# An adaptive layer and a routed feed-forward in one kernel: a third row buffer, another order of GpSimd's transfers, and no memsets between them

## The chip, the cores and the metric

One core of a Trainium2 chip. The time is that of one execution on the device, in microseconds (us), as median of several runs. The profile is one execution recorded by the hardware profiler; its times count from the span's start. Five engines work at the same time, each along its own queue of instructions: TensorE (PE), VectorE (DVE), ScalarE (ACT), GpSimd (POOL) and SyncE (SP). Semaphores alone order them.

## The reference

```python
def _L0_cond_ref(x, u, v, b, W, fc_bias):          # x (16, 512, 512); u = v (16, 1, 512, 16)
    z1 = einsum('bfi,bir->bfr', x, v[:, 0]) / inch
    z = einsum('bfr,bor->bfo', z1, u[:, 0]) / r
    return gelu(einsum('bfi,oi->bfo', x, W) + fc_bias + z + b)

def _L0_ffn_ref(x, w_router, b_router, w1, b1, w2, b2):   # 16 blocks of 128, 4 chosen for a row
    prob = softmax(xf @ w_router + b_router)
    _, idx = top_k(prob, 4)
    mask = (idx[:, :, None] == arange(16)).any(axis=1)
    h = relu(einsum('nd,ebd->neb', xf, w1b) + b1b)
    return einsum('neb,ebd,ne->nd', h, w2b, mask) + b2

x = x + _L0_ffn_ref(_L0_cond_ref(x, ...), ...)
```

There are 8192 rows of 512 numbers, all float32. A row's hidden values are needed for its four chosen blocks ("experts") alone.

## The kernel before

The rows are worked in 16 batches of 512, each in four quarters of 128 rows, so 64 steps. A step's layer (`layer`, three products of rounded high and low parts in place of a float32 product) ends in a PSUM bank; ScalarE takes it through gelu into a row buffer, `grow`. TensorE turns it (`turn_batch`), multiplies with the router's weights (`router`, partial sums over four chunks of 128 channels, which stand in four groups of 32 partitions), and for each batch the logits are copied to SBUF (`logits`) and turned to rows of tokens (`turn_logits`). VectorE chooses four experts for each row (`choose`, `choose_rest`), TensorE counts ahead of each row how many went to its expert (`ranks`), and VectorE makes from this the four places of the row in the experts' lists (`place`, semaphore `v_ix`).

GpSimd then scatters the row to its four places in DRAM (`place_rows`, tensor `xg`): four indirect DMAs for a quarter, each of 128 rows of 528 words (512 numbers, the row's number and other places). A row buffer may be overwritten when its scatters have landed (`s_sc`).

The lists are cut into tiles of 512 rows of one expert: 49 full tiles and 23 of two halves of 256, 72 in all. Tile `j` is loaded by SyncE from `xg` as soon as the batches that must be complete for it have landed (`load_tile`, `unlocked_by`): tile 41 needs batch 14, tile 45 batch 15. TensorE turns it (`turn_tile`), multiplies with the expert's first weights (`ffn1`, result `hid`), ScalarE and VectorE make from it the two parts of the hidden layer (`hh`, `hl`), and TensorE multiplies with the second weights (`ffn2`). ScalarE (even quarters) and VectorE (odd ones) copy the results out of PSUM into a result buffer `yss[n]` (`result`), and GpSimd scatters them, four indirect DMAs for a tile, into `yt` (`send`). A result buffer is free when its tile's scatters have landed (`s_y`).

All engines walk the same steps `s`. Step `s` does the layer of quarter `s` (to 63), the first product of tile `s - 30` and the second of tile `s - 31`; GpSimd in its step `s` places quarter `s - 7` and sends tile `s - 32`. The stages are thus: layers alone (steps 0 to 29), layers and tiles (30 to 63), tiles alone (64 to 102), and at the end VectorE adds four parts and `x` for each row, while SyncE loads and stores.

What stands in whose place in SBUF matters here. There are two row buffers `grow[0]` and `grow[1]`; the first six batches also use a third one in the space of `ys`. Result buffers 0 and 1 are `ys`, buffer 2 is `yspare` (in the space of the low parts of experts 8 to 11, `w2l[:, 8:12]`) up to tile 40, buffer 3 is `stx` from tile 36 on, buffers 4 and 5 are `grow[0]` and `grow[1]` from tiles 39 and 43 to 54, when batches 14 and 15 have been scattered. A tile takes of the free buffers the one longest unused. Up to tile 45 (`PRE`) the second weights are split for each tile; later tiles use splits of all experts (`presplit_w2`), which VectorE and ScalarE make two at a time in steps 67 to 72, 75 and 76, in the order of `PRESPLIT`.

Between two indirect DMAs of GpSimd stands a memset (`rest`), which waits for the memset before it. It writes 320 words a partition of `w2l[:, 15]`, or, in late steps, the small tile `rep`; expert 15's low part can be written only when 412 of them are done. From step 77 on there is instead one small memset after the second transfer of a tile, and a wait for it (`stop`).

```python
first = s <= LAG + 2 or q != 3
if 0 <= s - 7 < SLOTS and first:
    place_rows((s - 7) // 4, (s - 7) % 4)
if 0 <= j < NTILE:
    for c in range(chunks(j)):
        send(j, c)
if 0 <= s - 7 < SLOTS and not first:
    place_rows((s - 7) // 4, (s - 7) % 4)
```

## Time and profile before

| | us |
|---|---|
| median of 3 runs | 1148.82 (1147.45 to 1150.53) |
| the profiled execution | 1149.37 |
| its span | 1147.6 |
| TensorE busy | 865.1 (75%) |
| VectorE busy | 861.7 (75%) |
| GpSimd busy | 727.4 (63%) |
| ScalarE busy | 581.1 (51%) |

The time of an execution holds 1.8 us outside the span. Busy time says little by itself: TensorE has nothing to do in the last stage, the sums, which begin at about 933 us and last for the rest of the span.

### The profile page before, as it was taken

To read this page: it belongs to the slowest core of one execution; us is meant where nothing else is said; L and a number is where in the kernel's file an instruction comes from. 1 tells how busy PE (TensorE), PEld (TensorE's weight loads), DVE (VectorE), ACT (ScalarE), POOL (GpSimd) and SP (SyncE) were. 2 spreads that over 40 slices of the span, in tenths; PEclk is the share of its full clock that TensorE was granted. 3 is DMA by queue.
4 is the path that set the end of the run, shared out by engine and by line. 5 is a ranking of instruction groups with operands and counts; after the bars stand their busy time and mean duration, and the time that the engine had idled before them with its cause. 6 is when DMAs were issued, how large, how long until landed. Compare 5 with 4: busy or idle time off the path is not lost.

```text
span 1147.6 us, 18685 instructions
## 1 busy us (share of the span) xinstructions
PE 865.1 (75%) x4893; PEld 682.7 (59%) x4893; DVE 861.7 (75%) x2175; ACT 581.1 (51%) x1061; POOL 727.4 (63%) x1038
## 2 busy tenths in 40 slices
PE   8989989999999999999999876999999930000000
PEld 7757767777777776777777655788888820000000
DVE  4556666777687767767778974878998759987777
ACT  6535545756676575657657753766667610000000
POOL 1588888888888888888888897555555530000000
PEclk9989989999999999999999997999999965555555
DMA  6798679988899888988778887689987589999999
GB/s 188 262 330 299 236 270 334 310 293 298 288 314 305 289 285 300 312 282 297 265 276 313 302 289 262 245 296 342 317 282 243 192 313 425 425 427 429 426 432 378
DMA packets 103241, 354.88 MB, mean 309 GB/s; under 512 B 29961, under 2 KB 29961, under 8 KB 92384
## 3 DMA queue, kind: packets, MB, share of 16 engines
q1 hardware_dynamic: 59616, 217.22, 55.0%
q0 software_dynamic: 43424, 136.37, 30.3%
q8 instruction: 41, 0.67, 0.2%
q14 instruction: 64, 0.52, 0.1%
q10 hardware_dynamic: 96, 0.10, 0.0%
HBM read 200.47 MB, written 169.65 MB: 323 GB/s over the span
## 4 chain that ended last, share of the span: by engine, by line
PE 50%; DVE 14%; POOL 12%; DMA 11%; issue 7%; ACT 3%; another core or an unknown queue 2%; ACTq 0%; POOLq 0%; DVEq 0%; SPq 0%
PE lay L1185 12%; DMA w2l<-yt 9%; PE yps L1327 9%; PE hid L1294 8%; PE trn L1279 7%; POOL yt L563 4%; POOL xg L544 4%; PE hid L1299 4%; POOL w2l L528 3%; DVE stx L1040 3%; PE hid L1171 2%; PE trn L1206 2%; ACT gsb L643 2%; DMA outT<-ys 2%
## 5 line engine op out<-in xcount | busy, mean ns | idle before, releaser
L544 POOL DMA_INDIRECT xg<-grow,ix x224 | 226.7, 1012 | 70.2 <-issue 36.4
L817 DVE TENSOR_TENSOR gsb<-trn,gsb 128x512 fp32r<-128x512 f32 x239 | 162.4, 687 | 127.3 <-ACT gsb L643 75.2
L563 POOL DMA_INDIRECT yt<-ys,ids x170 | 176.7, 1039 | 72.6 <-issue 35.8
L1185 PE MATMUL lay<-w2l,xs 128*128 128x512 f32 x768 | 194.3, 403 | 0.0
L1279 PE MATMUL trn<-idf,gr 128*128 128x128 f32 x956 | 147.3, 277 | 27.0 <-DVE gsb L817 12.9
L1185 PEld LDWEIGHTS lay<-w2l,xs 128*128 128x128 f32 x768 | 144.6, 192 | 30.1
L528 POOL MEMSET w2l<- 128x320 f32 x412 | 161.3, 392 | 0.1
L1279 PEld LDWEIGHTS trn<-idf,gr 128*128 128x128 f32 x956 | 115.8, 142 | 68.3 <-DVE gsb L817 22.9
L643 ACT ACTIVATE gsb<-trn 128x512 fp32r<-128x512 f32 x239 | 142.6, 597 | 26.5 <-PE trn L1279 15.2
L1294 PE MATMUL hid<-gsb,w1c 128*128 128x512 f32 (+1 forms) x576 | 133.1, 374 | 11.9 <-ACT gsb L643 10.2
L671 ACT ACTIVATE hv<-hid,b1c 128x512 f32<-128x512 f32 (+1 forms) x94 | 52.6, 584 | 155.4 <-PE hid L1299 53.0
L1327 PE MATMUL yps<-w2c,hh 128*128 128x512 f32 x330 | 118.6, 441 | 3.1 <-DVE hl L1008 2.1
L1294 PEld LDWEIGHTS hid<-gsb,w1c 128*128 128x128 f32 x576 | 95.2, 192 | 39.3 <-ACT gsb L643 22.9
L1299 PE MATMUL hid<-gsb,w1c 128*128 128x512 f32 (+1 forms) x288 | 68.9, 362 | 3.8 <-DVE gsb L817 3.8
L626 ACT ACTIVATE grow<-lay 128x512 f32<-128x512 f32 x56 | 33.5, 598 | 66.1 <-PE lay L1190 43.6
L1327 PE MATMUL yps<-w2c,hl 128*128 128x512 f32 x165 | 65.8, 399 | 0.0
L563 POOL DMA_INDIRECT yt<-stx,ids x40 | 43.1, 1077 | 26.2 <-issue 9.5
L563 POOL DMA_INDIRECT yt<-yspare,ids x52 | 52.7, 1013 | 8.6 <-issue 8.1
L1299 PEld LDWEIGHTS hid<-gsb,w1c 128*128 128x128 f32 x288 | 50.4, 193 | 12.5 <-DVE gsb L817 4.2
L1327 PEld LDWEIGHTS yps<-w2c,hh 128*128 128x128 f32 x330 | 50.3, 193 | 7.3 <-DVE hl L1008 3.5
L795 DVE TENSOR_TENSOR xs<-stx,xs 128x512 fp32r<-128x512 f32 x64 | 44.1, 694 | 12.2 <-ACT xs L599 9.7
L635 ACT ACTIVATE stx<-trn 128x512 f32<-128x512 f32 x64 | 38.1, 595 | 30.0 <-remote 13.4
(243 smaller groups left out, 1823.9 us busy)
## 6 DMA issues: line engine op xcount, KB each, us to landing
gr<-xg SPq DMA_DIRECT2D x49, 1056.0 KB
xs<-yt SPq DMA_DIRECT2D x16, 2048.0 KB, 19.5
w2l<-yt SPq DMA_DIRECT2D x15, 2048.0 KB, 19.5
gr<-xg SPq DMA_DIRECT2D x45, 528.0 KB
stx<-xT SPq DMA_DIRECT2D x64, 256.0 KB, 4.3
outT<-ys SPq DMA_DIRECT2D x31, 512.0 KB, 20.4
xg<-xrow SPq DMA_DIRECT2D x16, 528.0 KB
w2f<-xrow SPq DMA_DIRECT2D x16, 512.0 KB
```

The source lines that it names most:

```text
L528: pool.memset(idle, 0.0).then_inc(g_pace, 1)
L544: pool.indirect_dma_start(out=xg, out_offset=bass.IndirectOffsetOnAxis(ap=ix[:, row_buffer(b), q, k:k + 1], axis=0), in_=grows[row_buffer( ...
L563: pool.indirect_dma_start(out=yt, out_offset=bass.IndirectOffsetOnAxis(ap=ids[:, j % 8, c:c + 1], axis=0), in_=yss[result_buffer(j)][:, c, ...
L643: act.activation(gsb[:, :, HI, c * P:(c + 1) * P], turned[TURN_BANK[n]][:, :].rearrange("p (k t) -> p k t", k=KC), ACT.Copy).then_inc(a_tn, 1)
L671: act.activation(hv[:, h * n:(h + 1) * n], hid[:, h * n:(h + 1) * n], ACT.Relu, bias=b1c[:, bass.DynSlice(e[h], 1)]).then_inc(a_hv, 1)
L795: dve.tensor_tensor(xs[:, b % 2, :, LO, cols], stx[:, x_buffer(s), :].rearrange("p (k t) -> p k t", k=KC), xs[:, b % 2, :, HI, cols].bitca ...
L817: dve.tensor_tensor(gsb[:, :, LO, c * P:(c + 1) * P], turned[TURN_BANK[n]][:, :].rearrange("p (k t) -> p k t", k=KC), gsb[:, :, HI, c * P: ...
L1185: pe.matmul(lay[s % 2][:, :], xs[:, b % 2, k, h, cols], wls[:, k, a, :], start=(k == 0 and a == HI and h == HI), stop=False)
L1279: last = pe.transpose(turned[TURN_BANK[n]][:, k * P:(k + 1) * P], gr[:, j % 2, c, k * P:(k + 1) * P], idf[:, :])
L1294: pe.matmul(hid[:, cols], w1x[h][:, a, k * P:(k + 1) * P], gsb[:, k, HI, cols], start=(h == 0 and k == 0 and a == HI), stop=False)
L1299: last = pe.matmul(hid[:, cols], w1x[h][:, HI, k * P:(k + 1) * P], gsb[:, k, LO, cols], start=False, stop=(h == len(parts) - 1 and k == KC ...
L1327: last = pe.matmul(second_out[RESULT_BANK[n]][:, :], hx[:, c * P:(c + 1) * P], w[a], start=(i == 0), stop=(i == 2))
```

## The change

The third row buffer (`grow3`) is there for all batches, so batch `b` is in buffer `b % 3`. It takes the space of the low parts of experts 11 to 14. The third result buffer is gone from there for tiles 0 to 33; `grow[1]` becomes one for tiles 34 to 54 (batch 13 was its last), `stx` from tile 36, the space of `grow3` for tiles 36 to 39 (now called buffer 5), `grow[0]` for tiles 39 to 54 (buffer 4, batch 15 was its last). GpSimd sends results ahead of rows in steps 33 to 66 and rows ahead of results before and after. Its memsets are gone up to step 76; the last three tiles have no pause either. The logits are turned by transposes of 128x128 with the identity `idf` into a whole bank, and VectorE sums the four chunks; before, a product with a matrix of ones (`sumk`) turned and summed at once. `PRE` is 47, and the splits for all experts go in the order 0 to 15.

```diff
-PRE = 46
-SPARE = 40
-MORE = 36, 39, 43, 55
+PRE = 47
+MORE = 34, 36, 39, 55
+SPARE = 36, 40
@@ row_buffer
-    return b % 3 if b < 6 else b % 2
+    return b % 3
@@ result_buffers
-        free = [0, 1] + [2] * (j <= SPARE) + [3] * (j >= MORE[0])
-        free += [4] * (MORE[1] <= j < MORE[3]) + [5] * (MORE[2] <= j < MORE[3])
+        free = [0, 1] + [2] * (MORE[0] <= j < MORE[3]) + [3] * (j >= MORE[1]) + [4] * (MORE[2] <= j < MORE[3])
+        free += [5] * (SPARE[0] <= j < SPARE[1])
@@ adaln_ffn
-        yspare = nc.alloc_sbuf_tensor_at("yspare", [P, 4, D], F32, offset=w2l_at + 8 * D * 4)
+        grow3 = nc.alloc_sbuf_tensor_at("grow3", [P, 4, W], F32, offset=w2l_at + 11 * D * 4)
+        yspare = nc.alloc_sbuf_tensor_at("yspare", [P, 4, D], F32, offset=w2l_at + 11 * D * 4)
-        yss = (ys[:, 0, :, :], ys[:, 1, :, :], yspare, stx, grow[:, 0, :, 0:D], grow[:, 1, :, 0:D])
+        yss = (ys[:, 0, :, :], ys[:, 1, :, :], grow[:, 1, :, 0:D], stx, grow[:, 0, :, 0:D], yspare)
@@ gpsimd
-            def rest(s):
-
-                if paced[0] > 0:
-                    pool.wait_ge(g_pace, paced[0])
-                idle = w2l[:, NE - 1, 0:REST].bitcast(F32) if s < SLOTS + 7 else rep[:, :, :].rearrange("p q e -> p (q e)")
-                pool.memset(idle, 0.0).then_inc(g_pace, 1)
-                paced[0] += 1
@@ place_rows
-                    rest(4 * b + q + 7)
@@ send
-                if j + LAG + 2 < PACED:
-                    rest(j + LAG + 2)
-                elif c == 1:
+                if j + LAG + 2 >= PACED and c == 1 and j < NTILE - 3:
                     stop()
@@ gpsimd's steps
-                first = s <= LAG + 2 or q != 3
+                first = s <= LAG + 2 or SLOTS + 3 <= s
@@ result, on scalar (and likewise on vector)
-                elif result_buffer(j) > 3:
-                    b = NB - 6 + result_buffer(j)
+                elif result_buffer(j) > 1:
+                    b = NB - 2 if result_buffer(j) == 5 else NB - 5 + result_buffer(j)
                     for q in range(4):
                         act.wait_ge(s_sc[row_buffer(b)][q], rows_sent(b))
@@ choose
-                lgs = rps[:, 256:256 + 4 * NE].rearrange("p (q e) -> p q e", q=4)
+                lgs = lexp
                 dve.wait_ge(p_lt, b + 1)
-                step(dve.tensor_reduce(lmax[:, :], lgs, AX.X, ALU.max))
+                step(dve.tensor_reduce(lgs[:, :, :], rps[:, :].rearrange("p (q k e) -> p q e k", q=4, k=KC)[:, :, 0:NE, :],
+                                       AX.X, ALU.add))
+                step(dve.tensor_reduce(lmax[:, :], lgs[:, :, :], AX.X, ALU.max))
@@ presplit_w2, on vector
-                if e == NE - 1:
-                    dve.wait_ge(g_pace, 4 * SLOTS + 4 * (SLOTS + 5 - LAG))
-                if e == 8:
-                    dve.wait_ge(s_y[2], results_sent(max(j for j in range(NTILE) if result_buffer(j) == 2)))
+                if e == 11:
+                    for q in range(4):
+                        dve.wait_ge(s_sc[2][q], rows_sent(NB - 2))
+                    dve.wait_ge(s_y[5], results_sent(max(j for j in range(NTILE) if result_buffer(j) == 5)))
@@ turn_logits
-                pe.wait_ge(g_s, KC + 1)
                 for q in range(4):
-                    last = pe.matmul(rps[:, 256 + q * NE:256 + (q + 1) * NE], lgT[:, q * P:(q + 1) * P], sumk[:, :],
-                                     start=True, stop=True)
+                    last = pe.transpose(rps[:, q * P:(q + 1) * P], lgT[:, q * P:(q + 1) * P], idf[:, :])
```

Where the instructions stand is read from the two programs. GpSimd, before, at steps 67 and 68: the first quarter of batch 15 (`xg<-grow`) is there with a memset behind each transfer (`yt<-` are results):

```order
797 L544 DMA xg<-grow,ix 102400x528
798 L528 MEMSET w2l 128x320
799 L544 DMA xg<-grow,ix 102400x528
800 L528 MEMSET w2l 128x320
801 L544 DMA xg<-grow,ix 102400x528
802 L528 MEMSET w2l 128x320
803 L544 DMA xg<-grow,ix 102400x528
804 L528 MEMSET w2l 128x320
```

GpSimd in the changed kernel, from the second-last quarter of batch 14 (`grow_49` is the third row buffer) over the four quarters of batch 15 (`grow`) to the results of tiles 39 and 40 (`yt<-grow`; tile 38's are the `ys` ahead of them):

```order
97 L529 DMA xg<-grow_49,ix 102400x528 x4
98 L547 DMA yt<-grow,ids 32768x512 x4
99 L529 DMA xg<-grow_49,ix 102400x528 x4
100 L529 DMA xg<-grow,ix 102400x528 x4
101 L547 DMA yt<-ys,ids 32768x512 x4
102 L529 DMA xg<-grow,ix 102400x528 x4
103 L547 DMA yt<-stx,ids 32768x512 x4
104 L529 DMA xg<-grow,ix 102400x528 x4
105 L547 DMA yt<-yspare,ids 32768x512 x4
106 L529 DMA xg<-grow,ix 102400x528 x4
107 L547 DMA yt<-ys,ids 32768x512 x4
108 L547 DMA yt<-grow,ids 32768x512 x8
```

From row 100 to row 106 there are 16 scatters of batch 15 and 12 of the results of tiles 35, 36 and 37. TensorE, before, at the end of a step in which the logits are turned (`rps` is the bank, `fu` holds the logits), ahead of the next layer:

```order
308 L1327 MATMUL yps<-w2c,hl 128x512
309 L1230 MATMUL rps<-sumk,fu 128x16 x4
310 L1185 MATMUL lay<-w2l,xs 128x512 x12
311 L1190 MATMUL lay<-w2l 128x512
312 L1206 MATMUL trn<-idf,grow 128x128 x4
```

And the same place in the changed kernel (its line 1206 is `turn_logits`):

```order
308 L1302 MATMUL yps<-w2c,hl 128x512
309 L1206 MATMUL rps<-idf,fu 128x128 x4
310 L1162 MATMUL lay<-w2l,xs 128x512 x12
311 L1167 MATMUL lay<-w2l 128x512
312 L1183 MATMUL trn<-idf,grow 128x128 x4
```

The place is the same, only the kind of product differs. VectorE's choice starts with one operation more in the changed kernel:

```order
173 L824 TENSOR_SCALAR fu<-rps,brc 128x512
174 L829 TENSOR_REDUCE lexp<-rps 128x64
175 L831 TENSOR_REDUCE lmax<-lexp 128x4
176 L832 TENSOR_TENSOR lsub<-lexp,lmax 128x64
```

## Rows read from the trace of the kernel before

**Rows 1.** Windows by stage: busy us (instructions) of each engine, then PEclk, DMA share, GB/s.

```profile
160.00:600.00 440.00, 419.98 (x2288) 326.50 (x2287) 321.16 (x980) 282.54 (x502) 390.58 (x563) 0.99 0.86 294
600.00:717.00 117.00, 93.92 (x472) 71.40 (x471) 89.96 (x246) 70.07 (x128) 100.41 (x146) 0.93 0.82 291
717.00:933.00 216.00, 204.17 (x1316) 173.83 (x1314) 177.12 (x370) 142.91 (x284) 123.96 (x141) 0.99 0.81 278
```

**Rows 2.** The chain of waits between 520 and 735 us: start, us, what.

```profile
539.17 1.16 POOL xg L544
...
683.81 0.39 POOL w2l L528
685.00 0.69 DVE gsb L817
```

**Rows 3.** Waits of GpSimd from 33 to 684 us: us in total, times, longest.

```profile
POOL xg L544 <- DVE ix L891: 34.8, 3, 33.1
```

**Rows 4.** Timeline of VectorE at the split of expert 15.

```profile
684.32 0.75 DVE L998 TENSOR_TENSOR w2l<-w2f,xs 128x512 fp32r<-128x512 f32 x1 [4.77 <-POOL w2l L528]
```

**Rows 5.** VectorE's `hl`, one for each tile, in three windows: ns min/median/max, first and last start.

```profile
L1008 DVE TENSOR_TENSOR hl<-hv,hh x9: 669/679/683, 599.5 to 674.0; 128x512 fp32r<-128x512 f32 x9
L1008 DVE TENSOR_TENSOR hl<-hv,hh x4: 675/680/682, 686.8 to 724.3; 128x512 fp32r<-128x512 f32 x4
L1008 DVE TENSOR_TENSOR hl<-hv,hh x26: 678/681/683, 724.3 to 920.5; 128x512 fp32r<-128x512 f32 x26
```

**Rows 6.** Windows around the stall, columns as in group 1.

```profile
679.50:685.00 5.50, 2.43 (x11) 1.67 (x9) 0.73 (x3) 1.78 (x4) 4.84 (x8) 1.00 0.83 274
...
704.00:717.00 13.00, 7.30 (x19) 5.43 (x20) 6.13 (x12) 5.25 (x10) 7.75 (x14) 0.50 0.57 205
```

**Rows 7.** Timeline of GpSimd in the middle stage.

```profile
310.39 0.38 POOL L528 MEMSET w2l<- 128x320 f32 x1
310.93 0.97 POOL L544 DMA_INDIRECT xg<-grow,ix  x1 [0.17 <-issue]
```

**Rows 8.** Timeline of GpSimd in the last tile stage.

```profile
749.96 0.98 POOL L563 DMA_INDIRECT yt<-ys,ids  x1 [0.98 <-POOL pace L533]
751.25 1.11 POOL L563 DMA_INDIRECT yt<-ys,ids  x1 [0.30 <-issue]
```

**Rows 9.** Timelines of VectorE and ScalarE: batch 15's places, tile 39's results.

```profile
629.90 0.75 DVE L891 TENSOR_SCALAR ix<-top 128x16 int32<-128x16 f32 x1
...
659.77 0.59 ACT L702 ACTIVATE grow<-yps 128x512 f32<-128x512 f32 x1
...
662.37 0.67 DVE L817 TENSOR_TENSOR gsb<-lay,gsb 128x512 fp32r<-128x512 f32 x1
```

**Rows 10.** GpSimd's timeline, SyncE's waits from 680 to 712 us, SyncE's timeline.

```profile
676.70 0.97 POOL L544 DMA_INDIRECT xg<-grow,ix  x1 [0.17 <-issue]
...
SPq L378 <- DMA xg<-grow,ix: 7.0, 1, 7.0
...
682.57 0.34 SPq L388 DMA_DIRECT2D gr<-xg  x1
```

**Rows 11.** The chain of waits between 395 and 450 us.

```profile
418.24 0.80 PE rps L1230 x8
...
422.13 0.44 PE trn L1206 x4
```

**Rows 12.** VectorE operations of 192 and 512 elements a partition.

```profile
L800 DVE TENSOR_TENSOR w2l<-fv,w2l x16: 340/350/379, 4.9 to 511.5; 128x192 fp32r<-128x192 f32 x16
L845 DVE TENSOR_SCALAR fu<-rps,brc x16: 749/750/754, 30.6 to 611.1; 128x512 f32<-128x512 f32 x16
```

**Rows 13.** ScalarE's timeline in the step of a choice.

```profile
422.21 1.28 ACT L626 ACT_TABLE_LOAD   x1 [0.54 <-PE lay L1190]
```

**Rows 14.** The chain of waits, and the timeline, in a step of the middle stage.

```profile
395.92 2.72 PE lay L1185 x12
...
406.72 2.73 PE lay L1185 x12
...
403.26 0.60 ACT L702 ACTIVATE yspare<-yps 128x512 f32<-128x512 f32 x1
...
407.43 0.68 DVE L1024 COPY yspare<-yps 128x512 f32<-128x512 f32 x1
```

More of the change, by code:

```diff
@@ L36 @@
 AHEAD = EARLY + 8
-REST = 320
 PACED = SLOTS + 13
-PRESPLIT = [*range(8), *range(12, NE), *range(8, 12)]
 ALU = mybir.AluOpType
@@ L112, in presplit_in @@
 def presplit_in(s):
-    n = 2 * (s - SLOTS - 3)
-    if s > SLOTS + 8:
-        n -= 4
-    return range(n, n + 2) if SLOTS + 3 <= s < SLOTS + 13 and s not in (SLOTS + 9, SLOTS + 10) else ()
+    n = s - SLOTS - 3
+    if n < 6:
+        return range(2 * n, min(2 * n + 2, 11)) if n >= 0 else ()
+    return range(2 * n - 5, min(2 * n - 3, NE)) if 8 <= n < 11 else ()
 def results_sent(j):
@@ L213, in adaln_ffn @@
         wrz = sb("wrz", [P, KC, 2 * NE], F32)
-        sumk = sb("sumk", [P, NE], F32)
         lmax = sb("lmax", [P, 4], F32)
@@ L514, in _ @@
             pool.iota(order[:, :], [[1, 2]], base=0, channel_multiplier=2).then_inc(g_k, 1)
-            pool.memset(sumk[:, :], 0.0).then_inc(g_s, 1)
-            for k in range(KC):
-                pool.wait_ge(g_s, k + 1)
-                pool.affine_select(out=sumk[:, :], in_=sumk[:, :], compare_op=ALU.not_equal, fill=1.0, base=-2 * NE * k,
-                                   pattern=[[-1, NE]], channel_multiplier=1).then_inc(g_s, 1)
-            paced = [0]
-            def rest(s):
-                if paced[0] > 0:
-                    pool.wait_ge(g_pace, paced[0])
-                idle = w2l[:, NE - 1, 0:REST].bitcast(F32) if s < SLOTS + 7 else rep[:, :, :].rearrange("p q e -> p (q e)")
-                pool.memset(idle, 0.0).then_inc(g_pace, 1)
-                paced[0] += 1
+            paced = [0]
             def stop():
@@ L728, in _ @@
                     split_w2(j - 1, expert[j - 1][0])
-                for n in presplit_in(s):
-                    presplit_w2(PRESPLIT[n])
+                for e in presplit_in(s):
+                    presplit_w2(e)
                 if s == KC + 1 or q == 2 and 2 <= b <= NB:
@@ L1016, in result @@
                     dve.wait_ge(p_r, SLOTS // 2)
-                elif result_buffer(j) > 3:
-                    b = NB - 6 + result_buffer(j)
+                elif result_buffer(j) > 1:
+                    b = NB - 2 if result_buffer(j) == 5 else NB - 5 + result_buffer(j)
                     for q in range(4):
                         dve.wait_ge(s_sc[row_buffer(b)][q], rows_sent(b))
-                if j == 1 or (j == 0 and c == 3):
-                    for q in range(4):
-                        dve.wait_ge(s_sc[2][q], rows_sent(5))
                 dve.tensor_copy(yss[result_buffer(j)][:, c, :], second_out[RESULT_BANK[4 * j + c]][:, :]).then_inc(v_y, 1)
```

28 lines of the change are left out of this document (12 added, 16 removed).

## The prediction

> **What bounds the kernel now.** I read the windows by stage first. In the middle stage (layer, routing and the tiles of the second part together) TensorE is busy for 95% of the time, in the last tile stage for 94%; between them, from 600 to 717 us, only for 80%, while GpSimd is busy for 86% [rows 1]. That middle piece is where a change of GpSimd's work can be worth something, so I read the chain of waits there: it goes along GpSimd's queue from 539.17 to 683.81 us without a break and leaves it through a memset, for VectorE [rows 2]. The waits say the same of the whole first part: from 33 to 684 us GpSimd waited for VectorE's places three times, 34.8 us in all, and 33.1 of that was the wait for the first batch [rows 3]. GpSimd is thus saturated for 640 us, but what others lose by it is met in one place: VectorE reaches the split of expert 15's second weights, whose low half is the memsets' scratch, and stands idle for 4.77 us until the last of 412 memsets is done [rows 4]. Before that GpSimd's queue is late, and nobody needs it sooner.
>
> What the place costs is read from `hl`, which VectorE makes once for each tile. From 599.5 to 674.0 us nine of them make 9.3 us a tile; from 674.0 to 724.3 four more take 50.3 us; afterwards 25 intervals take 196.2 us, 7.85 each [rows 5]. At 7.85 the four would take 31.4, so 18.9 us are lost there: 4.8 in the wait and 14.1 behind it. The 14.1 go with TensorE's clock: in 704 to 717 us the granted clock is 0.50, the lower of its two levels (1.2 GHz), after 5.5 us in which TensorE was busy for 2.43 [rows 6].
>
> **No memsets between transfers.** A transfer costs GpSimd 0.97 us, the memset 0.38, the gap behind it 0.17: 1.52 [rows 7]. Where a transfer follows a transfer the gap is 0.30 [rows 8], so 0.97 + 0.30 = 1.27. The change frees 412 x 0.25 = 103 us of GpSimd's time. None of it is on the chain before 539 us. At the split of expert 15 the wait for memsets is gone, and with it what hangs behind: -18.9 us, if nothing takes its place. The five instructions for `sumk` at the start lie before the first batch is ready, which GpSimd awaits anyway [rows 3]: 0.
>
> **What takes its place.** GpSimd's order from tile 35 on and the new result buffers have to be read together. Tile 39 gets buffer 4, which is row buffer 0; before, that held batch 14, now it holds batch 15, the last one. ScalarE must not write tile 39 before all 16 scatters of batch 15 have landed. They can't start before the places of batch 15, at 629.90 us [rows 9]. The order shows four groups of scatters with three groups of results between them: 28 transfers, so the last begins 27 x 1.27 = 34.3 us later, at 664.4 (with GpSimd still in the group before, at most 2.3 us more: VectorE works these steps without a gap, so its times should stand). The last scatter of batch 15 began at 676.70 us, and SyncE's load that waited 7.0 us for it was issued at 682.5: 5.8 us to land [rows 10]. That makes 670.2 to 672.5. ScalarE wants to write tile 39 at 659.77, and the work behind it in its queue, `gsb` of the next tile, is taken by VectorE 2 us later, at 662.37 [rows 9]. The stall is 8.4 to 10.7 us; I take 10. Queued behind ScalarE's waiting copy are the last quarter of `gsb`, the hidden layer of tile 40 and so TensorE. What the stall does to the clock no row shows for this place: nothing is the one end (VectorE's 9.3 us a tile leave 1.45 over TensorE's 7.85), 14.1 us as now the other. I take the middle, 7. So the piece from 600 to 717 us gives 18.9 - 10 - 7 = 1.9 us.
>
> One rule speaks on the landing. The row gives 5.8 us from the start of the issue to the release of the load. The Trainium skill ("DMA: Bandwidth & Descriptors", section on the anatomy of one DMA, SWDGE path) fits 2.0 us + bytes / 436e3; for 128 rows of 2112 B, 270 KB, an estimate from that page is 2.6 us. By it the stall would be 3.2 us shorter and the sum 1138.3. The row is longer because other transfers are in flight; the sum goes by the row.
>
> **Transposed logits.** On TensorE eight records (four true fp32 products) of 0.80 us become four transposes, and a set of four takes 0.44 in the chain [rows 11]; 0.36 us less, sixteen times, in stages where the chain is mostly TensorE's: -5.8 us. VectorE gets a sum over 256 PSUM elements a partition in each batch ahead of the maximum. The trace has no reduction of that size; by the ops of 192 and 512 elements, 0.350 and 0.750 us [rows 12], it is 0.35 + 64 x 0.4 / 320 = 0.43 us (bounds 0.35 and 0.75). It delays `lsub` and ScalarE's exponential. ScalarE has 0.54 us there in which it waits for the layer before it loads its table [rows 13], so I cost it at 0. Without that cover it is 16 x 0.43 = 6.9 us.
>
> **Third row buffer, two result buffers.** The third buffer relaxes a wait (gelu on the scatters of two batches back, now three) that the chain does not hold: 0. It takes the place of the third result buffer for tiles 0 to 33. Cover of that: the last result of a tile is ready at 408.11 us, 1.4 after the next layer began at 406.72; results go out first now, so it lands some 5.8 us behind its issue, at about +9.8 with 2.6 us of queue. The buffer is wanted again at +10.8 (a layer step, 395.92 to 406.72) + 7.3 (ScalarE's first result, 403.26, against 395.92), +18.1 [rows 14]. Spare: 8.3 us a tile: 0. PRE 47, the other order of the early splits and the skipped pause of the last tiles move one 0.7 us split by a step: 0.
>
> **Sum.** -5.8 - 1.9 = -7.7 us against the profiled execution's 1149.4 us (span 1147.6): 1141.7. The median of the runs is 0.55 us lower, so I say 1141.
>
> **Rivals.**
> Forecast, 0.40: as above, 1133 to 1146.
> No wait for batch 15, 0.17: GpSimd or the landing is quicker than the rows say, or these steps of the second part are slower. Then both parts of 18.9 come home: 1149.4 - 5.8 - 18.9 = 1124.7. For it: 14.1 of the 18.9 are clock and not work. Against it: 28 transfers can't be passed.
> The wait drags the clock as now, 0.17: 1149.4 - 5.8 - 18.9 + 10 + 14.1 = 1148.8, no change. For it: a stall of half the length did so in this trace.
> The longer choice is not covered, 0.10: 1141.7 + 6.9 = 1148.6, no change. For it: the step of the choice already has TensorE waiting for `gsb`.
> Two result buffers are too few, 0.16, the one that ends slower: ScalarE and VectorE wait for the landing of the tile two before. It decides when issue and landing of four results take 8.3 us longer than reckoned, for instance because eight transfers now go out back to back and SyncE's loads lie between them. Each us over that costs about 32 us in 32 tiles: 1173 at 1 us, 1157 at half. Against it: GpSimd needs 8 x 1.27 = 10.2 us in a step of 12.5 and is not behind.
>
> **How the numbers follow.** A measurement of this kernel tells 0.3%, 3.4 us, from no change. Faster: nearly all of the forecast (0.38) and the case without the wait (0.17), 0.55. Same: the clock, the choice and the rest of the forecast, 0.29. Slower: the result buffers, 0.16. The range for 8 in 10 is 1122 to 1157: from the case without the wait to half a us a tile in the last; the forecast's own is 1133 to 1146.
>
> **What would show it.** GpSimd's transfers 1.27 us apart and GpSimd idle in the middle stage, waiting for results. ScalarE (its copy of tile 39) idle for about 10 us, released by a scatter of batch 15, then a stretch at granted clock 0.5. No wait for a memset ahead of the split of expert 15. TensorE's transposes of the logits near 0.44 us for four, the new reduction near 0.43. In the middle stage about 0.36 us less a batch, and no copy of results waiting for its buffer; such waits, or longer steps in the middle stage, would make the prediction wrong, and so would a tile 39 that does not wait.

## The result, and where the time went

The changed kernel takes 1274.63 us (median of 4 runs, 1271.19 to 1279.31), the kernel before 1149.4 us beside it: ratio 1.1114, 95% interval 1.1093 to 1.1135. That is 125 us slower where 8 us faster was forecast. (All ratios here and below compare fast runs alone; of the four runs with memsets of 80 words one was slow.) The page of the profile after, its parts 1, 2 and 4:

```profile
span 1277.5 us, 17997 instructions
PE 886.4 (69%) x4829; PEld 696.1 (54%) x4829; DVE 851.1 (67%) x2192; ACT 580.5 (45%) x1062; POOL 557.8 (44%) x594
PEclk9988878989999999999999896999999996555555
PE 45%; another core or an unknown queue 16%; DVE 12%; DMA 11%; issue 8%; ACT 5%; ACTq 2%; SPq 1%; POOLq 0%; DVEq 0%; POOL 0%
```

GpSimd lost its memsets and is busy for 44% of a longer span. Nothing took its place as a busy engine: TensorE's share fell too, to 69%. New is the 16% of the chain that the page puts on another core or a queue it can't name; it was 2% before. The windows by stage, columns as in [rows 1]: the layers alone, then the three stages of [rows 1], cut where this kernel is in them:

```profile
33.00:233.00 200.00, 138.72 (x682) 101.97 (x681) 87.45 (x438) 74.18 (x129) 94.08 (x96) 0.83 0.63 222
233.00:700.00 467.00, 404.63 (x2133) 314.01 (x2132) 296.58 (x921) 266.86 (x476) 254.28 (x255) 0.96 0.74 254
700.00:845.00 145.00, 110.60 (x545) 84.64 (x543) 98.01 (x282) 76.79 (x141) 83.26 (x82) 0.88 0.71 253
845.00:1053.00 208.00, 199.40 (x1294) 170.20 (x1293) 176.03 (x371) 141.51 (x282) 116.63 (x129) 0.99 0.81 277
```

In the last row nothing changed: TensorE is busy for 96% of it, 95% in [rows 1]. The loss lies ahead of it, where GpSimd sends rows. Nearly half is lost before tile 0: the products that end its hidden layer (first and last start of the group, in the kernel before and then in this one) begin at

```profile
L1299 PE MATMUL hid<-gsb,w1c x8: 389/393/395, 174.0 to 185.5; 128*128 128x512 f32 x8
```

```profile
L1274 PE MATMUL hid<-gsb,w1c x4: 389/389/397, 232.3 to 233.0; 128*128 128x512 f32 x4
```

That is 58 us by tile 0. In the first window TensorE works 139 of 200 us; it is not short of clock alone (0.83), it stands still. Who waits, 33 to 800 us (some of the rows):

```profile
...
POOL yt L547 <- ACT ys L681: 140.6, 60, 12.2
POOL xg L529 <- DVE ix L872: 121.0, 10, 37.0
ACT hv L653 <- remote: 89.4, 24, 9.3
...
ACT grow L608 <- remote: 47.0, 6, 13.8
...
ACT stx L617 <- remote: 34.6, 12, 5.0
```

GpSimd now waits for places (121.0 us in ten waits, where [rows 3] had 34.8 in three) and for results: others keep it waiting. Ahead of them stands ScalarE, which waits for something the trace calls remote, a releaser that it can't name, on operations that read what TensorE has just made (`grow` from the layer, `stx` from the turned batch, `hv` from the hidden layer). One such place, in the timelines of TensorE, ScalarE, VectorE and GpSimd:

```profile
141.34 0.60 PE L1183 MATMUL trn<-idf,grow 128*128 128x128 f32 x4
...
144.54 0.39 PE L1167 MATMUL lay<-w2l 98*128 98x512 f32 x1
151.34 1.08 PE L1198 MATMUL rps<-stx,wrz 128*32 128x256 f32 x8 [6.40 <-issue]
...
145.14 0.60 ACT L608 ACTIVATE grow<-lay 128x512 f32<-128x512 f32 x1 [5.45 <-PE lay L1167]
150.69 0.60 ACT L617 ACTIVATE stx<-trn 128x512 f32<-128x512 f32 x1 [4.95 <-remote]
...
157.17 0.60 ACT L608 ACTIVATE grow<-lay 128x512 f32<-128x512 f32 x1 [5.12 <-remote]
...
157.20 0.75 DVE L824 TENSOR_SCALAR fu<-rps,brc 128x512 f32<-128x512 f32 x1 [4.34 <-remote]
...
153.73 0.96 POOL L529 DMA_INDIRECT xg<-grow,ix  x1 [0.30 <-issue]
166.69 0.96 POOL L529 DMA_INDIRECT xg<-grow,ix  x1 [12.00 <-DVE ix L872]
```

The layer's last product is in the record at 144.54 + 0.39 us. ScalarE's gelu, which waits for it, starts at 157.17: 12.2 us later, of which ScalarE stands idle for the last 5.1. The turned batch of 141.34 is read at 150.69. The router's product ends at 151.34 + 1.08, and VectorE's copy of the logits, which waits for that product alone, starts 4.8 us behind it, at 157.20, together with the gelu. So it is not the row buffer that gelu waits for: the logits go into none. Meanwhile GpSimd issues its transfers 1.27 us apart, the last of the batch at 153.73. A signal that doesn't come from TensorE passes at once in the same stretch: ScalarE's `stx` ends at 151.29 and TensorE's product with it starts at 151.34. So what is late is TensorE's completions as the others see them, while GpSimd issues without a pause. 2.5 us after GpSimd's last transfer has ended they are there, VectorE makes the places, and GpSimd starts the next 16 transfers (166.69), with 12.00 us lost on its own queue. That is the ring: late completions, late places, an idle GpSimd. Behind the first batch's wait for places, 37.0 us, nine more make 84.0. On the chain of waits the unnamed queue stands between two pieces of TensorE's work again and again:

```profile
301.49 1.48 PE rps L1198 x8
303.00 1.43 another core or an unknown queue
304.48 3.64 another core or an unknown queue
```

### The profile page after: what moved, and what is told of

Same layout as the page of the kernel before. It is cut to its first block, busy times and chain, and to the rows that moved or that the text cites. A ratio compares the mean times of both kernels' runs of the same rounds, so it can differ in the third digit from the quotient of the medians.

```text
span 1277.5 us, 17997 instructions
## 1 busy us (share of the span) xinstructions
PE 886.4 (69%) x4829; PEld 696.1 (54%) x4829; DVE 851.1 (67%) x2192; ACT 580.5 (45%) x1062; POOL 557.8 (44%) x594
## 4 chain that ended last, share of the span: by engine, by line
PE 45%; another core or an unknown queue 16%; DVE 12%; DMA 11%; issue 8%; ACT 5%; ACTq 2%; SPq 1%; POOLq 0%; DVEq 0%; POOL 0%
PE lay L1162 11%; DMA w2l<-yt 8%; PE yps L1302 8%; PE trn L1254 7%; PE hid L1269 6%; PE hid L1274 3%; DVE stx L1017 2%; DVE gsb L796 2%; ACT gsb L625 2%; PE trn L1183 2%; PE hid L1148 2%; DMA outT<-ys 2%; PE lay L1302 1%; PE rps L1198 1%
## 5 line engine op out<-in xcount | busy, mean ns | idle before, releaser
L529 POOL DMA_INDIRECT xg<-grow,ix x256 | 251.7, 983 | 198.4 <-DVE ix L872 121.0
L547 POOL DMA_INDIRECT yt<-ys,ids x212 | 219.0, 1033 | 232.9 <-ACT ys L681 148.4
L1254 PE MATMUL trn<-idf,gr 128*128 128x128 f32 x956 | 153.9, 286 | 74.5 <-DVE gsb L796 68.3
L1162 PE MATMUL lay<-w2l,xs 128*128 128x512 f32 x768 | 199.0, 410 | 0.0
L1254 PEld LDWEIGHTS trn<-idf,gr 128*128 128x128 f32 x956 | 120.6, 146 | 118.9 <-DVE gsb L796 85.1
L1269 PE MATMUL hid<-gsb,w1c 128*128 128x512 f32 (+1 forms) x576 | 137.3, 382 | 6.3 <-ACT gsb L625 5.6
L1302 PE MATMUL yps<-w2c,hh 128*128 128x512 f32 x334 | 124.2, 454 | 5.1 <-issue 4.1
L608 ACT ACTIVATE grow<-lay 128x512 f32<-128x512 f32 x64 | 38.2, 597 | 118.3 <-PE lay L1167 63.3
L1274 PE MATMUL hid<-gsb,w1c 128*128 128x512 f32 (+1 forms) x288 | 69.4, 364 | 0.0
L1001 DVE COPY ys<-yps 128x512 f32<-128x512 f32 x90 | 61.0, 680 | 3.5 <-PE yps L1302 1.8
L681 ACT ACTIVATE ys<-yps 128x512 f32<-128x512 f32 x87 | 52.2, 600 | 9.1 <-PE yps L1302 5.3
```

The lines of the kernel that those rows point to most:

```text
L529: pool.indirect_dma_start(out=xg, out_offset=bass.IndirectOffsetOnAxis(ap=ix[:, row_buffer(b), q, k:k + 1], axis=0), in_=grows[row_buffer( ...
L547: pool.indirect_dma_start(out=yt, out_offset=bass.IndirectOffsetOnAxis(ap=ids[:, j % 8, c:c + 1], axis=0), in_=yss[result_buffer(j)][:, c, ...
L681: act.activation(yss[result_buffer(j)][:, c, :], second_out[RESULT_BANK[4 * j + c]][:, :], ACT.Copy).then_inc(a_y, 1)
L1001: dve.tensor_copy(yss[result_buffer(j)][:, c, :], second_out[RESULT_BANK[4 * j + c]][:, :]).then_inc(v_y, 1)
L1162: pe.matmul(lay[s % 2][:, :], xs[:, b % 2, k, h, cols], wls[:, k, a, :], start=(k == 0 and a == HI and h == HI), stop=False)
L1254: last = pe.transpose(turned[TURN_BANK[n]][:, k * P:(k + 1) * P], gr[:, j % 2, c, k * P:(k + 1) * P], idf[:, :])
```

## The experiments

Theory H, held back: GpSimd's transfers, issued with only 0.30 us between them, hold TensorE's completions back, and the memset's pause prevented it. Rivals: B, the two result buffers, the third row buffer and the order of results and rows; L, the transposed logits. The kernels were run in five sets, each on another chip, and each ratio is to the kernel before on the same chip. It took 1149, 1149 and 1146 us on three of the chips (sets 1, 3 and 4) and 1133 and 1130 us on the other two (sets 2 and 5). That difference turned out to matter.

### Set 1: the memsets alone, and the others without them

The kernel before without its memsets, and without the wait of expert 15's split for them:

```diff
-                    rest(4 * b + q + 7)
-                if j + LAG + 2 < PACED:
-                    rest(j + LAG + 2)
-                elif c == 1:
+                if j + LAG + 2 >= PACED and c == 1:
                     stop()
```

> The kernel before with one edit of the change alone: no memset behind GpSimd's transfers (the few memsets from step 77 on stay). Theory H (held back): while GpSimd issues transfers with only 0.30 us between them, TensorE's completion signals reach the other engines microseconds late, and the memset's pause is what prevents it. H expects 1250 to 1290 us: the change lost 126 us in all, 58 us up to tile 0's first layer of the experts, about 8 us per batch in the middle stage and 12 us behind it. Theory B (buffers and order): the loss comes from two result buffers, the third row buffer and results ahead of rows, which this kernel does not have, so it expects 1130 to 1149 us, the memsets' stalls being gone. Theory L (transposed logits) expects the same as B.

Measured: 1297.24 us, 1.1321 (1.1257 to 1.1385). One edit out of the whole change gives more than the whole loss.

The changed kernel with the memsets back:

```diff
+                pool.memset(w2l[:, NE - 1, 64:64 + REST].bitcast(F32), 0.0).then_inc(g_pace, 1)
```

> The changed kernel with the memset of 320 words behind each transfer put back (up to step 76, in the part of the last expert's weights that the third row buffer leaves free), every other edit of the change kept. H expects 1130 to 1155 us: the loss of 126 us goes with the memsets' return, and what remains is the sum of the other edits (logits 5.8 us less, the wait at tile 39 up to 10 us more). B and L expect 1240 us or more, since what they blame is all still there.

Measured: 1146.63 us, 0.9992 (0.9965 to 1.002). All 125 us are back, with both result buffers, the third row buffer and the transposed logits in place. B and L are out as causes of the loss. B's buffers do show: seven times ScalarE's copy of a result waits for its buffer (`ys`, for the scatters of the tile before in it), 12.0 us in all, a wait that neither the trace of before nor that of the changed kernel has. The same place in a batch, in its timelines of TensorE and ScalarE:

```profile
131.84 0.39 PE L1180 MATMUL lay<-w2l 98*128 98x512 f32 x1
...
132.33 0.60 ACT L619 ACTIVATE grow<-lay 128x512 f32<-128x512 f32 x1 [1.58 <-PE lay L1180]
```

Gelu starts 0.1 us behind the layer's last product (131.84 + 0.39, then 132.33) where it started 12.2 us behind. Over the whole program ScalarE and VectorE wait for a remote releaser for 5.3 us here, and for 243.8 us in the changed kernel. The kernel before is not free of it: its trace has 63.9 us, the first of them ahead of tile 0.

The kernel before with the transposed logits alone:

```diff
-                    last = pe.matmul(rps[:, 256 + q * NE:256 + (q + 1) * NE], lgT[:, q * P:(q + 1) * P], sumk[:, :],
+                    last = pe.transpose(rps[:, q * P:(q + 1) * P], lgT[:, q * P:(q + 1) * P], idf[:, :])
```

> The kernel before with the transposed logits alone (four transposes and an addition on VectorE in place of eight products), memsets and buffers as before. H expects 1143 us: 0.72 us less on TensorE per batch, 16 times gives at most 11.5, half of it on the chain as in the prediction. L expects 1200 us or more. B expects 1143 to 1149 us.

Measured: 1151.48 us, 1.0027 (1.0002 to 1.0053): no gain, where every theory but L had 1149 or less. The saving on TensorE is the prediction's 0.36 us a batch, not the 0.72 put down here. In the timeline the eight products of before and the four transposes of this kernel differ by 0.36 us, first the row of before, then this kernel's:

```profile
418.08 0.96 PE L1230 MATMUL rps<-sumk,fu 128*128 128x16 f32 x8
```

```profile
417.36 0.60 PE L1231 MATMUL rps<-idf,fu 128*128 128x128 f32 x4
```

Its chain by engine, its scatters from 600 us on (ns min/median/max, first and last start), and a wait of ScalarE over the whole program:

```profile
PE 28%; POOL 23%; DMA 18%; DVE 13%; issue 9%; ACT 3%; SPq 3%; another core or an unknown queue 1%; ACTq 0%; DVEq 0%; POOLq 0%
```

```profile
L544 POOL DMA_INDIRECT xg<-grow,ix x24: 966/966/1411, 606.2 to 675.4; - x24
```

```profile
ACT grow L626 <- DMA xg<-grow,ix: 69.4, 20, 8.3
```

They say why it is worth nothing: GpSimd is 23% of the chain, the last scatter of batch 15 starts at 675.4 us (676.70 in [rows 10]), and gelu waits twenty times, 69.4 us in all, for a row buffer whose scatters haven't landed. With memsets of 320 words GpSimd, saturated, sets the pace of the middle stage, and the layer runs into it. With the third row buffer (the kernel above) that wait is 5.7 us, and the time is still GpSimd's.

A memset of 4 words in place of 320, otherwise as the changed kernel with memsets:

> As the changed kernel with memsets back, but each memset writes 4 words in place of 320, so that GpSimd's pause is shorter by most of the memset's 0.38 us (period some 1.30 in place of 1.52 us) and the instruction still stands between the transfers. H in the form 'the length of the pause decides' expects near the changed kernel's time, 1230 us or more. H in the form 'any instruction between two transfers lets the signals through' expects within 5 us of the kernel with 320 words.

Measured: 1272.28 us, 1.1087 (1.1045 to 1.1128), as the changed kernel without any. The timeline of GpSimd:

```profile
149.58 0.97 POOL L537 DMA_INDIRECT xg<-grow,ix  x1 [0.19 <-issue]
150.54 0.12 POOL L521 MEMSET w2l<- 128x4 f32 x1
150.85 0.97 POOL L537 DMA_INDIRECT xg<-grow,ix  x1 [0.19 <-issue]
```

The small memset fits into the gap that is there anyway, the transfers stay 1.27 us apart. An instruction between them is not what helps.

### Set 2: how long a pause

The changed kernel with memsets of 160, 240 and 448 words (each with its own number):

```diff
-REST = 320
+REST = 160
```

and one without long memsets:

```diff
+            def rest():
+                sent[0] += 1
+                if sent[0] % 3 == 0:
+                    stop()
```

> The changed kernel with memsets of 160 words behind the transfers (those of 4 words gave 1272 us, those of 320 gave 1147 us). Period of a transfer worked out as 0.97 + about 0.27 + 0.17 = 1.41 us. Theory 'threshold' (GpSimd's transfers fill something that takes a fixed time for each of them, above 1.31 us): below it signals pile up, so between 1160 and 1250 us, by how near 1.41 is. Theory 'any real pause is enough': GpSimd, which with 320 words sets the pace of the middle stage (32 transfers of 1.52 us are 48.6 of 50 us per batch), gets faster, and the kernel with it: 1135 to 1147 us.

> The same with memsets of 240 words, period worked out as some 1.47 us. Threshold: between the kernels with 160 and 320 words. Any real pause: 1138 to 1147 us.

> The same with memsets of 448 words, period worked out as 0.97 + 0.50 + 0.17 = 1.64 us. If signals are already on time at 1.52 us, a longer pause only makes GpSimd slower: 32 transfers per batch of 52.5 in place of 48.6 us, 3.8 us for each of some 10 batches from step 30 to step 71, 1180 to 1190 us. If signals are still late at 1.52 us, part of that comes back, 1150 to 1175 us.

> The changed kernel with no memset behind each transfer, but behind every third one a memset of 4 words and a wait for it, which the trace shows as 0.14 + 0.98 us. Three transfers take 1.27 + 1.27 + 2.1 = 4.6 us, a mean of 1.55 us, so the mean pace is that of the kernel with 320 words and two of three gaps are the short ones. If the mean rate of transfers decides: 1145 to 1165 us. If each gap has to be long: 1230 us or more.

Measured: 160 words 1100.12 us, 0.9705 (0.9665 to 0.9744); 240 words 1117.58 us, 0.9854 (0.9811 to 0.9898); 448 words 1183.68 us, 1.0458 (1.0413 to 1.0502); the wait behind every third transfer 1102.41 us, 0.9737 (0.9684 to 0.9791). On this chip nothing is held back at 160 words: none of the four traces has a wait of ScalarE or VectorE for a remote releaser. Every further word only slows GpSimd. 448 words fall in the range put down, but it was reckoned from another chip's 1147 us, and the kernel with 320 words was not run here, so that agreement is in part luck; the other three came out below every time put down for them. The wait behind every third transfer is short in this stretch, 0.28 us and not the 0.98 of [rows 8], so the transfers went out faster than meant, 1.27, 1.27 and 1.36 us apart where nothing else delays them. Its timeline of GpSimd, its chain by engine, and a wait from 600 to 720 us:

```profile
150.87 0.96 POOL L537 DMA_INDIRECT xg<-grow,ix  x1 [0.30 <-issue]
151.83 0.12 POOL L526 MEMSET pace<- 128x4 f32 x1
152.23 0.97 POOL L537 DMA_INDIRECT xg<-grow,ix  x1 [0.28 <-POOL pace L526]
```

```profile
PE 65%; DMA 15%; DVE 9%; issue 5%; POOL 4%; ACT 2%; SPq 0%; ACTq 0%; POOLq 0%; DVEq 0%
```

```profile
ACT grow L692 <- DMA xg<-grow,ix: 17.7, 1, 17.7
```

With GpSimd off the chain (4%, TensorE 65%) the wait of the prediction shows, in the last line: ScalarE's copy of tile 39 for the scatters of batch 15, 17.7 us. With 320 words (set 1) it was 24.3 us, and there the last scatter of batch 15 started at 674.7:

```profile
ACT grow L692 <- DMA xg<-grow,ix: 24.3, 1, 24.3
```

```profile
L537 POOL DMA_INDIRECT xg<-grow,ix x28: 966/969/1426, 600.8 to 674.7; - x28
```

### Set 3: the same questions on another chip

Memsets of 80 words (`REST = 80`), and memsets of 160 words behind every third transfer with no wait for them:

```diff
+                sent[0] += 1
+                if sent[0] % 3:
+                    return
```

> The changed kernel with memsets of 80 words behind the transfers: 4 words (period 1.27 to 1.31 us) gave 1272 us, 160 words (1.38 us) gave 0.9705 of the kernel before. The memset of 80 words takes 0.20 us, so the period is 0.97 + 0.20 + 0.17 = 1.34 us. Theory 'threshold between 1.31 and 1.38 us, sharp': either within 10 us of the kernel with 160 words, or over 1240 us. Theory 'gradual' (each 0.05 us of pause gives back part of the signals' delay): about 1180 us.

> The changed kernel with a memset of 160 words behind every third transfer only, and no wait for it: gaps of 0.30, 0.30 and 0.41 us, so a mean period of 1.31 us, which is nearly that of the kernel with a 4-word memset and a wait for it behind every third transfer (1.27, 1.27 and 1.36 us; 0.974 of the kernel before). Theory 'pace': what matters is a pause of some 0.1 us now and then, and this is about as fast as that kernel, under 1130 us. Theory 'drain': what matters is that GpSimd's queue once waits for its own engine to be done, which only the wait brings; then this one loses as the changed kernel did, 1230 us or more.

The kernel before with one number changed:

```diff
-REST = 320
+REST = 160
```

> The kernel before with its memsets shortened from 320 to 160 words and nothing else changed. If the gain of the kernel with 160 words in the changed layout (0.9705 of before) is all GpSimd's shorter pause: 0.965 to 0.975 of before here as well. If the changed kernel's other edits carry it (they measured 0.9992 together with 320 words): 0.99 or more. Both partly: 0.975 to 0.985. The wait of 18 us at tile 39, which only the changed layout has, would make this one the faster, 0.955 to 0.965.

The last of the set takes the late buffer later:

```diff
-MORE = 34, 36, 39, 55
+MORE = 34, 36, 41, 55
```

> The changed kernel with the 4-word memset and wait behind every third transfer, and with the result buffer in batch 15's row buffer taken from tile 41 on in place of 39. In the kernel without the second edit (0.974 of before) TensorE waits 18.0 us once at tile 39 for a result copy that waits for batch 15's transfers. If that wait is on the chain by its full length: 0.958 to 0.962 of before. If GpSimd's results are late anyway: 0.970 to 0.975.

Measured: 80 words 1251.36 us, 1.0842 (1.0745 to 1.0938); 160 words behind every third transfer 1245.53 us, 1.0845 (1.0811 to 1.0878); the kernel before with 160 words 1244.04 us, 1.0802 (1.0745 to 1.0859); wait behind every third transfer and buffer from tile 41, 1220.46 us, 1.0602 (1.0548 to 1.0657). The last two fell outside all that was expected, and against set 2: there both recipes had gained 3%. The first two fell where 'sharp threshold' and 'drain' had them, but both theories were set up against set 2's times, which this chip doesn't give, so they decide nothing yet. In the last kernel the completions of TensorE are late again, from 33 to 190 us:

```profile
POOL xg L537 <- DVE ix L883: 74.7, 6, 36.7
ACT grow L619 <- remote: 22.0, 3, 9.6
```

Either these edits made the difference, or the chip did.

### Set 4: chip or kernel

The changed kernel with no edit, and the one with `REST = 160` of set 2 with no other:

> The changed kernel unaltered, beside the three others of this set. The set with memsets of 160, 240 and 448 words had the kernel before at 1133 us, the other sets at 1149 us, so they ran on different chips. Theory 'chip' (on the chip with 1133 us signals are held back less or not at all, so the good results of 160 words and of the wait behind every third transfer are that chip's): here, if the kernel before is at 1149 us, 1.11 of it; if it is at 1133 us, clearly less than 1.11, down to 0.97. Theory 'kernel' (the edits themselves made those differences): 1.11 whatever the chip.

> The changed kernel with memsets of 160 words, as it measured 0.9705 beside a kernel before of 1133 us. Theory 'chip': on a chip where the kernel before takes 1149 us, 1.05 or more, as the kernel before with 160 words did (1.080). Theory 'kernel' (the third row buffer and the order make 160 words enough): 0.97 on any chip.

The other two have `REST = 240` and `REST = 320`, and both

```diff
-MORE = 34, 36, 39, 55
+MORE = 34, 36, 41, 55
```

> Memsets of 240 words (period about 1.46 us), and the result buffer in batch 15's row buffer from tile 41 on. If the period at which signals come through lies between 1.38 and 1.46 us here: 0.97 to 0.985 of before, by the shorter middle stage (0.06 us for each of some 430 transfers, up to 26 us, and less where TensorE becomes the bound). If it lies above 1.46 us: over 1.02.

> Memsets of 320 words and the later result buffer. With the wait at tile 39 the same kernel was 0.9992 of before, and it ended that stage with GpSimd's last results at 689.7 us as the kernel before did, TensorE's gain of 10 us up to step 68 being lost. If the wait at tile 39 held the chain: 0.985 to 0.992. If GpSimd's queue holds it (pace 1.52 us): 0.995 to 1.001.

Measured: the changed kernel again 1274.34 us, 1.1102 (1.1058 to 1.1147); 160 words, the very kernel of set 2, 1205.99 us, 1.053 (1.0474 to 1.0585); 240 words and tile 41 1163.78 us, 1.0145 (1.0106 to 1.0184); 320 words and tile 41 1138.61 us, 0.9942 (0.9924 to 0.9961). The changed kernel again fits both theories; 160 words decide for 'chip'. 240 and 320 words each fell just between the two ranges put down for them. The kernel with 160 words on the two chips, window from 33 to 190 us, first set 2, then here, with the waits for a remote releaser that only this run has:

```profile
33.00:190.00 157.00, 145.32 (x805) 108.79 (x806) 109.76 (x500) 89.47 (x156) 131.32 (x213) 0.99 0.88 317
```

```profile
33.00:190.00 157.00, 122.74 (x632) 90.03 (x631) 81.33 (x407) 66.09 (x116) 110.02 (x176) 0.89 0.72 252
```

```profile
ACT grow L619 <- remote: 14.3, 4, 6.3
ACT stx L628 <- remote: 12.6, 5, 5.0
```

One kernel, the same 1.38 us between transfers, and TensorE's completions are late on one chip and on time on the other. So it is the chip, as far as one set on each can tell it from the hour. On the chips where the kernel before takes 1146 to 1149 us the results can be put in order by the mean distance of GpSimd's transfers in 45 to 190 us (starts to starts, those under 2.5 us). The last column is the sum of ScalarE's and VectorE's waits for a remote releaser in the whole trace:

| transfers of the changed kernel | mean distance, us | ratio to before | waits for remote, us |
|---|---|---|---|
| no memset (both measurements) | 1.29 | 1.111, 1.110 | 243.8, 234.2 |
| 4 words | 1.31 | 1.109 | 250.2 |
| 160 words behind every third | 1.34 | 1.085 | 190.7 |
| 80 words | 1.35 | 1.084 | 198.3 |
| wait behind every third, tile 41 | 1.36 | 1.060 | 157.2 |
| 160 words | 1.42 | 1.053 | 112.1 |
| 240 words, tile 41 | 1.49 | 1.015 | 74.9 |
| 320 words | 1.54 | 0.999 | 5.3 |
| 320 words, tile 41 | 1.54 | 0.994 | 5.9 |

It is gradual, and the loss goes with the waits. 160 words behind every third transfer and 80 words behind each cost the same, as do their mean distances. The wait behind every third lies off the row, 2.4% better at 1.36 us than 80 words at 1.35, so a wait may do more than its length; that was not followed up. The kernel before lies off it too: it lost 13.2% without memsets (1.30 us) and 8.0% at 160 words (1.41 us).

The last kernel of the table is faster than the one with 320 words and tile 39, and than the kernel before: its wait for batch 15, in the copy that now stands at tile 41, is 7.6 us in place of 24.3:

```profile
ACT grow L692 <- DMA xg<-grow,ix: 7.6, 1, 7.6
```

### Set 5: transfers or bytes, and the late steps of before

```diff
-        xg = nc.dram_tensor("xg", (LREG * NE, W), F32, kind="Internal").ap()
+        xg = nc.dram_tensor("xg", (LREG * NE, WN), F32, kind="Internal").ap()
...
-                        in_=grows[row_buffer(b)][:, q, :], in_offset=None).then_inc(s_sc[row_buffer(b)][q], 16)
+                        in_=grows[row_buffer(b)][:, q, D // 2:W], in_offset=None).then_inc(s_sc[row_buffer(b)][q], 16)
```

> The changed kernel (no memsets), with the rows' transfers moving only the second half of each row and its ids, 1,088 in place of 2,112 bytes, and the loads of tiles reading as much; the number of transfers and of their rows stays. The first half of each token stays whatever lay there, so the output is not the layer's. Theory 'issue' (what holds TensorE's signals back is how often GpSimd starts a transfer): still over 1.08 of the kernel before, the stalls of 12 to 15 us per batch before step 30 still there. Theory 'traffic' (the bytes in flight hold them back): below 1.03 of before, stalls gone.

Measured: 1089.4 us, 0.9637 (0.9607 to 0.9667). GpSimd's transfers are 1.27 us apart, and ScalarE waits for TensorE only in the ordinary way (a row of GpSimd's timeline, then ScalarE's longest wait from 33 to 190 us):

```profile
105.25 0.96 POOL L530 DMA_INDIRECT xg<-grow,ix  x1 [0.30 <-issue]
```

```profile
ACT grow L609 <- PE lay L1169: 38.2, 22, 2.8
```

But this set ran on a chip with the kernel before at 1130 us, near the 1133 of set 2, where nothing was held back at mean distances of 1.38 us and more, and the changed kernel with whole rows was not run on either. The run shows that transfers 1.27 us apart hold nothing back by themselves on such a chip when they carry 1,088 bytes a row. Whether bytes or the chip made that, it leaves open.

The kernel before with 320 words from step 71 to 76:

```diff
-                idle = w2l[:, NE - 1, 0:REST].bitcast(F32) if s < SLOTS + 7 else rep[:, :, :].rearrange("p q e -> p (q e)")
+                idle = w2l[:, NE - 1, 0:REST].bitcast(F32) if s < SLOTS + 7 else fu[:, 0:REST]
```

> The kernel before with one edit: from step 71 to 76 its memsets write 320 words (in a buffer that is idle then) in place of 80, so that the pause is as long there as before step 71. The prediction put down 14.1 us at steps 73 to 76 to the clock after a wait. If they are signals held back behind transfers 1.34 us apart, the kernel gains 8 to 14 us: 0.988 to 0.993 of before. If they are the clock's, nothing changes: 0.998 to 1.002, or slower by the longer memsets.

Measured: 1129.39 us, 0.9997 (0.998 to 1.0013), by the number the 'clock' case. VectorE's split of expert 15 waited 14.5 us for the memsets here (4.77 us in [rows 4]), which ate what the later steps may have gained:

```profile
DVE w2l L1001 <- POOL w2l L531: 14.5, 1, 14.5
```

The windows behind that wait speak against the clock all the same (columns as in [rows 1]):

```profile
682.00:686.00 4.00, 3.95 (x13) 3.22 (x14) 3.16 (x8) 1.28 (x2) 3.51 (x6) 0.56 0.78 313
686.00:697.00 11.00, 11.00 (x61) 8.55 (x59) 7.96 (x16) 7.70 (x15) 9.57 (x13) 1.00 0.70 238
```

Three times as long a wait left TensorE at a granted clock of 0.56 for 4 us, then at 1.00 and busy without a gap. The trace has no wait for a remote releaser at all, so on this chip nothing was held back that longer memsets could free. The run doesn't tell what 80 words do on a chip of the other kind.

## Why the prediction was wrong

**The step that failed** is "No memsets between transfers": "The change frees 412 x 0.25 = 103 us of GpSimd's time. None of it is on the chain before 539 us." I priced the memset by the time it takes and by who waits for GpSimd, and found both free. It was the pause in GpSimd's stream of transfers, and on these chips the others see TensorE's completions late without it (5.3 us of waits for a remote releaser with it, 243.8 without). Taken out alone it costs 13.2%, put back alone it returns everything. None of the five cases had it; the nearest, "two result buffers are too few", had eight transfers back to back in it and priced them at up to 1 us a tile. That case didn't cause the loss: with memsets the copies did wait for their buffers, 12.0 us in seven waits, but the kernel took no longer (0.9992).

**The sign was there.** The kernel before has such a piece, the steps with memsets of 80 words, which the prediction read in [rows 5, 6]: 14.1 us lost behind the split of expert 15, put down to TensorE's clock. But between the wait and the stretch at 0.50 lies one at full clock:

```profile
693.00:704.00 11.00, 6.96 (x36) 5.09 (x34) 3.78 (x10) 3.23 (x6) 9.40 (x15) 0.99 0.84 297
```

So the low clock stands behind other stops. TensorE stood still again, for 4.66 and 5.08 us ahead of 704.62 and 712.09, and from 690 to 730 us ScalarE waited for the same unnamed releaser, on the operations that read TensorE's results:

```profile
ACT hv L671 <- remote: 6.9, 1, 6.9
...
ACT gsb L643 <- remote: 6.2, 3, 4.4
```

By the table above, 80 words hold TensorE back. That this is what cost the 14.1 us is argued from the trace and from the runs with 80 words elsewhere; the run that was to show it in place ran on a chip where nothing is held back.

**The wait at tile 39** doesn't occur in the changed kernel: no copy in its trace waits for batch 15's scatters. ScalarE's first copy of tile 39 starts at 803.05 us, 10.5 behind the last scatter (792.54), for TensorE and ScalarE are later still than GpSimd. The wait was right in kind and short in size for the kernels with a pause: 8.4 to 10.7 us were reckoned, 17.7 and 24.3 were measured. Two slips in the working cancel: the places are there at 629.90 + 0.75, and 662.37 is 2.6 us behind 659.77, not 2; with both the same 8.4 to 10.7 come out. The sum by the page's fit would be 1138.5, not 1138.3. Why the row's 5.8 us are longer than that fit, no run shows. With the pause kept, the last scatter started at 674.7 us where 664.4 was reckoned without it, and where GpSimd was faster (17.7 us) TensorE and ScalarE were at tile 39 sooner too, which the reckoning, on before's times, left out. Moved to tile 41 the wait is 7.6 us and the kernel half a per cent faster (0.9992 to 0.9942, but on two chips).

**Transposed logits**: 0.36 us a batch on TensorE and 0.42 us for the sum on VectorE (0.43 forecast), both as reckoned:

```profile
159.16 0.42 DVE L829 TENSOR_REDUCE lexp<-rps 128x64 f32<-128x256 f32 x1 [1.21 <-PE rps L1206]
```

Their -5.8 us on the end was wrong, because with memsets the chain of the middle stage was GpSimd's and not TensorE's. I had written that GpSimd is "saturated for 640 us" and then let TensorE's saving through. On set 2's chip, with TensorE on the chain, the changed layout gains 3% at 160 words; how much of it is the logits' and how much the shorter pause's was not measured, for the kernel before with 160 words was not run there.

**The other edits** (row buffer, order) were put at 0. With memsets of 320 words they are within the measurement, though each does something: with the third row buffer gelu's wait is 5.7 us in place of 69.4, and the two result buffers bring one of 12.0. Where completions are late the changed layout loses less than the kernel before. On set 1's chip it lost 10.9% with 4 words, at 1.31 us, and the kernel before 13.2% at 1.30; on set 3's chip it lost about as much at 1.35 us (1.084) as the kernel before at 1.41 (1.080). Which of the edits helps was not measured.

**What would show it** named "such waits, or longer steps in the middle stage" as what would make the prediction wrong, but of copies for their buffer; the waits that came were for TensorE. It also named a tile 39 that does not wait, and that came. GpSimd idle in the middle stage came as well, but because others were late and not because it was ahead.

The profile's own end of a product is no evidence of when it was done. The Trainium skill ("Perfetto Trace Analysis", section "Tensor Engine Instruction (MATMUL, LD_WEIGHTS)") says that the reported end is computed from the instruction's size, and that the signal is sent when PSUM has acknowledged the last bytes. The case agrees in that 12.2 us lie between such an end and its reader, and 4.8 us where nothing but the product is waited for. So it can't be said whether the array, its writes or its signals are held back; only that everything behind TensorE sees it late, and what comes from ScalarE in the same stretch doesn't.

## What to carry to other kernels

An instruction that computes nothing may be there for its time: before it is taken out of a queue of back-to-back transfers, take it out alone and measure, and look in the trace for a stretch that lacks it. Time saved on an engine is worth nothing where another one's queue is saturated through the stage; follow the saving to the next place where the two meet. And tune such a pause on more than one chip: the length that gained 3% on one cost 5% on another.

## What the runs showed of the hardware that was not expected

TensorE's completions reached ScalarE 12.2 us late in the place shown, while GpSimd issued indirect transfers of 128 rows of 2,112 bytes 1.27 us apart. The DMA engines were not full then: their mean share was 0.63 from 134 to 145 us and 0.56 from 145 to 155, against 0.88 over the layers where 160 words ran freely. The loss falls with the mean distance of the transfers, from 11% at 1.29 us to none at 1.54, and the waits for a remote releaser fall with it, from 244 to 5 us. Chips differ: with 160 words one lost 5.3% and one gained 3.0%, with the kernel before 1.1% quicker on the second, and none of the six traces from the two quicker chips has such a wait. Open are which part of the chip holds the completions, and whether transfers or their bytes count.
